# Waiting for every four or five gathers before the next are issued, in a DLRM tower with a compressed interaction network

## The chip, the core and the metric

The kernel runs on one core of a Trainium2 chip. The time is device microseconds from start to end of one execution. The core has a matrix engine (PE, TensorE), a vector engine (DVE, VectorE), an activation engine (ACT, ScalarE), GpSimd (POOL), a queue engine (SP, SyncE) and 16 DMA engines. Each engine runs its own list of instructions, and they meet through semaphores.

## The reference

```python
e = stack([tbl_f[ids[:, f]] for f in range(26)], axis=1)      # (512, 26, 32), tables of 1000 to 125000 rows
x1 = einsum('bik,bjk,hij->bhk', e, e, W1) + b1                # W1 (128, 26, 26)
x2 = einsum('bik,bjk,hij->bhk', x1, e, W2) + b2               # W2 (128, 128, 26)
z = sum(concatenate([x1, x2], axis=1), axis=-1)               # (512, 256)
h = relu(concatenate([z, dense_ctx], axis=1) @ W_top1 + b_top1)   # 272 -> 512
h = relu(h @ W_top2 + b_top2)                                 # 512 -> 256
y = h @ W_top3                                                # (512, 1)
```

Everything is in float32.

## The kernel before

**Batch tiles.** The 512 samples are four tiles of 128. For each tile, GpSimd gathers the 26 embedding rows of its 128 samples: 26 indirect DMAs (L199), each of which brings 128 rows of 128 bytes (one per partition) from one table. The four tiles' buffers `rows[t]` are separate, so no gather waits for a consumer. GpSimd does nothing else after two short instructions (L190, L192): it waits for the indices (`s_idx`) and issues 104 gathers in one go. Each gather adds 16 to `s_got[t][part]`. The fields are in three parts, `PARTS`: 0 to 12, 13 to 22, 23 to 25.

**Setup.** Weights come in over SP's and ACT's queues. Meanwhile and afterwards W1 and W2 are folded into one weight set, independent of the samples. PE walks a list of 37 steps, `SETUP`: 13 steps `fold` (four matmul records each, L219), 5 steps `ctA` and 5 `ctB` (L224, six records each, the last of either two), then transposes `v0` and `v1` (L230, L233). Each step writes one of seven PSUM banks (`RING`), adds 1 to `s_su`, and ACT evicts it (`take`, L345 to L359) and adds 1 to `s_sf`; PE waits for the eviction seven steps back. DVE adds terms of the evicted weights (`add`, L497): first after all 13 folds, then after `ctA`, then after `ctB`.

**A tile.** `half_a(t)` on DVE waits for part 0 (L450), transposes it (L451), copies it (L457), spreads it (L459) and forms products (L608 to L613). `half_b(t)` does so with parts 1 and 2 and makes eight products (L623). PE's `moments(t)` (L252, L253) start with the first of these, in 4 steps that ACT (`evict`, L373 and L381) and DVE (`bands`, L486) evict. Then come `z2_low`, `z2_high`, `z1` (L259 to L272), `layer1(t)` (L283 to L288), and, inside the next tile or at the end, `layer2` (L298) and `layer3` (L305). DVE's order is: setup sums of the folds and of `ctA`, `half_a(0)`, sums of `ctB`, `half_b(0)`, `bands(0)`, and then for each tile `half_a`, `half_b`, `bands`.

Of the kernel before, what the change touches and what calls it, by code (L numbers as in the profile page):

```python
# [71 lines left out]


PARTS = [(0, 13, COL_A), (13, 23, COL_B), (23, 26, COL_B + 10)]

WARM = 24
D_CTX = 16
# [18 lines left out]
def dlrm_tower(nc, io, tables, out):  # L96
    with ExitStack() as ctx:
# [3 lines left out]
        def sem(name):  # L101
            return ctx.enter_context(nc.semaphore(name))
# [40 lines left out]
        s_got = [[sem(f"s_got{t}_{part}") for part in range(3)] for t in range(TILES)]  # L143
# [31 lines left out]
        @block.sync  # L175
        def _(sp):
            sp.dma_start(idx[:, 0, :], io["ids"][:, 0, :]).then_inc(s_idx[0], 16)
            sp.dma_start(w1p[:], io["w1p"]).then_inc(s_w1p, 16)
            sp.dma_start(idx[:, 1:TILES, :], io["ids"][:, 1:TILES, :]).then_inc(s_idx[1], 16)
            sp.dma_start(w2t[:, 0:HALF, :], io["w2t"][:, 0:HALF, :]).then_inc(s_w2, 16)  # L180
            sp.dma_start(wt1[:], io["W_top1"][0:2 * H, :].rearrange("(c p) n -> p c n", p=P)).then_inc(s_wt, 16)
            sp.dma_start(wt1c[:], io["W_top1"][2 * H:2 * H + D_CTX, :]).then_inc(s_wt, 16)
            sp.dma_start(wt2[:], io["W_top2"].rearrange("(c p) n -> p c n", p=P)).then_inc(s_wt, 16)
            sp.wait_ge(s_y, TILES)
            sp.dma_start(out.rearrange("(o b) c -> o (b c)", o=1), y[:]).then_inc(s_out, 16)
            sp.wait_ge(s_out, 16)

        @block.gpsimd
        def _(pool):
            nc.gpsimd.memset(ones[:], 1.0).then_inc(s_ident, 1)  # L190
            pool.wait_ge(s_ident, 1)
            nc.gpsimd.affine_select(out=ident[:], in_=ones[:], compare_op=ALU.is_equal, fill=0.0, base=0,  # L192
                                    pattern=[[-1, P]], channel_multiplier=1).then_inc(s_ident, 1)
            for t in range(TILES):
                if t < 2:
                    pool.wait_ge(s_idx[t], 16)
                for part, (f0, f1, _) in enumerate(PARTS):
                    for f in range(f0, f1):
                        pool.indirect_dma_start(  # L199
                            rows[t][:, f, :], None, tables[f],  # L200
                            bass.IndirectOffsetOnAxis(ap=idx[:, t, f:f + 1], axis=0)).then_inc(s_got[t][part], 16)

        @block.tensor
        def _(pe):
# [212 lines left out]
        def _(dve):  # L417
# [28 lines left out]
            def fields_in(t, part):  # L446

                f0, f1, col = PARTS[part]
                n = f1 - f0
                dve.wait_ge(s_got[t][part], 16 * n)  # L450
                nc.vector.transpose(prod[:, :, col:col + n].rearrange("p g f -> p f g"),  # L451
                                    rows[t][:, f0:f1, :]).then_inc(s_turn[part], 1)
                dve.wait_ge(s_turn[part], t + 1)
                if part == 1:
                    dve.wait_ge(s_pa, t + 1)
                first = f0 % HALF
                nc.vector.tensor_copy(factor[:, :, first:first + n], prod[:, :, col:col + n]).then_inc(s_fac, 1)  # L457
                for r in range(QUADS):
                    nc.vector.tensor_scalar(diag[:, :, f0:f1, r], prod[:, :, col:col + n], quad[:, r:r + 1], None, ALU.mult)  # L459

            def half_a(t):
                if t:
                    dve.wait_ge(s_mom, t * STEPS)
                fields_in(t, 0)
                dve.wait_ge(s_fac, t * len(PARTS) + 1)
                products_a(nc.vector, prod, factor).then_inc(s_pa, 1)

            def half_b(t):
# [4 lines left out]
                dve.wait_ge(s_dup, t + 1)  # L473
                dve.wait_ge(s_fac, (t + 1) * len(PARTS))
                for s in range(PRODS):
# [126 lines left out]
def products_a(eng, prod, factor):  # L602

    def field(f, n=1):
        return prod[:, :, COL_A + f:COL_A + f + n]

    for col, o, d, n in PC + PD:
        eng.tensor_tensor(prod[:, :, col:col + n], factor[:, :, o:o + n], field(o + d, n), ALU.mult)  # L608
    eng.tensor_tensor(prod[:, :, PCD:P11].rearrange("p g (c d) -> p g c d", d=D[1]),
                      with_dims(factor[:, :, C[0]:], (HALF, GROUPS), (1, C[1]), (0, D[1])),  # L610
                      with_dims(field(D[0]), (PCOLS, GROUPS), (0, C[1]), (1, D[1])), ALU.mult)
    for x, col in ((JLOW, P11), (JLOW + 1, P12)):
        ins = eng.tensor_tensor(prod[:, :, col:col + x + 1], factor[:, :, 0:x + 1],  # L613
                                with_dims(field(x), (PCOLS, GROUPS), (0, x + 1)), ALU.mult)
    return ins
# [84 lines left out]
```

## Time and profile before

| | us |
|---|---|
| median of 3 runs | 290.71 (289.09 to 292.08) |
| the profiled execution | 289.82 |
| its span, first to last instruction | 288.1 |
| mean granted clock of TensorE | 0.738 of full speed |

Busy time over the span: PE 161.0 us (56%), DVE 97.5 us (34%), ACT 56.7 us (20%), GpSimd 100.1 us (35%). No engine is busy for much more than half of the span, so the averages do not say what bounds the kernel. The slices of the page and the chain of waits do: the first says when each engine works, the second what released it.

### The profile page before, as it was taken

The numbers are of one execution on the slowest core, as the hardware profiler recorded it, in microseconds if no ns is written. First come the engines' busy times: TensorE is split into PE (matmuls) and PEld (weight loads), VectorE is DVE, ScalarE is ACT, GpSimd is POOL, SyncE is SP. The second block draws the span as 40 slices with busy tenths as digits, with TensorE's granted clock in tenths as the row PEclk, the third lists the DMA queues.
The fourth block names the chain that finished last, engine by engine and source line by source line (L and its number), as shares of the span: only waits on it lengthen the run. The fifth ranks groups of instructions, "written<-read, shape, count | busy, mean of one in ns | idle before, by whom it ended". The sixth has DMA issues, their size and how long they took to land.

```text
span 288.1 us, 3079 instructions
## 1 busy us (share of the span) xinstructions
PE 161.0 (56%) x1193; PEld 146.8 (51%) x1193; DVE 97.5 (34%) x341; ACT 56.7 (20%) x156; POOL 100.1 (35%) x110
## 2 busy tenths in 40 slices
PE   8764221121111111111114449799999999999996
PEld 8753221011010101011014339799999999999995
DVE  2400000000000302100019996499249826973100
ACT  1021000000000000000032423602450245026312
POOL 5777777777777777774000000000000000000000
PEclk9995555555555555555555769979999999999999
DMA  6910110001101101100000000000000000000000
GB/s 228 354 17 12 14 15 14 12 14 14 14 12 14 14 11 15 14 13 9 0 0 0 0 0 3 1 2 0 2 0 2 0 2 1 2 0 2 2 0 0
DMA packets 5217, 5.97 MB, mean 21 GB/s; under 512 B 2226, under 2 KB 4402, under 8 KB 5203
## 3 DMA queue, kind: packets, MB, share of 16 engines
q0 software_dynamic: 3328, 1.71, 4.2%
q1 hardware_dynamic: 1410, 2.52, 2.7%
q10 hardware_dynamic: 464, 1.54, 1.5%
q8 instruction: 9, 0.15, 0.2%
q14 instruction: 6, 0.04, 0.0%
HBM read 5.77 MB, written 0.00 MB: 20 GB/s over the span
## 4 chain that ended last, share of the span: by engine, by line
PE 42%; another core or an unknown queue 35%; DVE 8%; issue 8%; ACT 3%; DMA 3%; SPq 0%
PE bank L252 12%; PE bank L253 6%; PE bank L259 5%; PE bank L263 4%; DVE folded L497 4%; PE bank L219 3%; DMA w2t<-in_w2t_dram 3%; PE bank L266 3%; PE bank L298 3%; PE bank L285 2%; PE bank L283 2%; ACT folded L345 1%; DVE diag L459 1%; PE bank L288 1%
## 5 line engine op out<-in xcount | busy, mean ns | idle before, releaser
L199 POOL DMA_INDIRECT rows<-in_tbl_dram,idx x104 | 99.4, 956 | 32.9 <-issue 31.4
L224 PE MATMUL bank<-w1s,w2t 128*128 128x169 f32 x52 | 21.9, 473 | 100.4 <-issue 97.1
L224 PEld LDWEIGHTS bank<-w1s,w2t 128*128 128x128 f32 x52 | 14.5, 301 | 107.4 <-issue 103.6
L252 PE MATMUL bank<-diag,prod 128*128 128x108 f32 x256 | 49.3, 293 | 1.4 <-DVE prod L623 1.4
L497 DVE TENSOR_TENSOR folded<-folded 128x6 f32<-128x6 f32 (+15 forms) x44 | 5.6, 177 | 108.6 <-issue 99.5
L252 PEld LDWEIGHTS bank<-diag,prod 128*128 128x128 f32 x256 | 38.8, 192 | 1.8 <-ACT v L351 1.8
L253 PE MATMUL bank<-diag,prod 128*77 128x64 f32 x256 | 36.9, 226 | 0.0
L253 PEld LDWEIGHTS bank<-diag,prod 128*77 128x77 f32 x256 | 30.9, 148 | 0.0
L486 DVE COPY t<-bank 13x128 f32<-13x128 f32 (+1 forms) x64 | 16.8, 263 | 31.7 <-PE bank L253 31.0
L345 ACT COPY folded<-bank 128x366 f32<-128x366 f32 x13 | 6.0, 465 | 84.1 <-remote 65.4
L373 ACT COPY t<-bank 55x256 f32<-55x256 f32 (+2 forms) x48 | 14.1, 294 | 28.2 <-PE bank L253 27.9
L497 DVE TENSOR_TENSOR folded<-folded,ct 128x52 f32<-128x52 f32 (+13 forms) x51 | 11.2, 299 | 24.5 <-ACT ct L348 24.5
L459 DVE TENSOR_SCALAR diag<-prod,quad 128x416 f32<-128x416 f32 (+2 forms) x48 | 16.9, 467 | 0.0
L259 PE MATMUL bank<-t,v 128*128 128x128 f32 x104 | 14.3, 301 | 1.8 <-ACT t L381 1.8
L348 ACT COPY ct<-bank 128x507 f32<-128x507 f32 (+1 forms) x10 | 4.7, 548 | 53.2 <-remote 36.1
L381 ACT COPY t<-bank 128x432 f32<-128x432 f32 x32 | 14.8, 514 | 0.0
L259 PEld LDWEIGHTS bank<-t,v 128*128 128x128 f32 x104 | 13.5, 213 | 2.5 <-ACT t L381 2.5
L623 DVE TENSOR_TENSOR prod<-bank,prod 128x364 f32<-128x364 f32 x32 | 14.5, 525 | 0.0
L219 PE MATMUL bank<-w1s,w2t 128*128 128x183 f32 x52 | 10.8, 359 | 6.4 <-issue 4.4
L230 PE MATMUL bank<-ident,folded 128*128 128x128 f32 x26 | 6.0, 422 | 13.1 <-DVE folded L497 13.1
L219 PEld LDWEIGHTS bank<-w1s,w2t 128*128 128x128 f32 x52 | 9.0, 210 | 7.9 <-issue 7.5
L263 PE MATMUL bank<-t,v 128*128 128x128 f32 x104 | 12.6, 278 | 0.0
(55 smaller groups left out, 168.3 us busy)
## 6 DMA issues: line engine op xcount, KB each, us to landing
rows<-in_tbl_dram,idx POOLq DMA_INDIRECT x104
wt<-in_W_top_dram SPq DMA_DIRECT2D x2, 512.0 KB
w2t<-in_w2t_dram ACTq DMA_DIRECT2D x1, 832.0 KB
w2t<-in_w2t_dram SPq DMA_DIRECT2D x1, 832.0 KB
w1t<-in_w1t_dram ACTq DMA_DIRECT2D x1, 640.0 KB
w1p<-in_w1p_dram SPq DMA_DIRECT2D x1, 521.0 KB
idx<-in_ids_dram SPq DMA_DIRECT2D x1, 39.0 KB
dctx<-in_dctx_dram ACTq DMA_DIRECT2D x1, 32.0 KB
```

The lines of the kernel that those rows point to most:

```text
L199: pool.indirect_dma_start(rows[t][:, f, :], None, tables[f], bass.IndirectOffsetOnAxis(ap=idx[:, t, f:f + 1], axis=0)).then_inc(s_got[t][p ...
L219: mm = nc.tensor.matmul(ps[:, i * PAIRS:(i + 1) * PAIRS], w2t[:, x0 + i, :], w1s[:, 0:PAIRS], start=True, stop=True)
L224: mm = nc.tensor.matmul(ps[:, i * CROSS:(i + 1) * CROSS], w2t[:, lo + x0 + i, :], w1s[:, c0:c0 + CROSS], start=True, stop=True)
L252: nc.tensor.matmul(m0[:, a0:a0 + JW * QUADS], prod[:, G, 0:P], mov, start=True, stop=True)
L253: mm = nc.tensor.matmul(m1[0:M1, a1:a1 + J1 * QUADS], prod[:, G, P:P + M1], mov[:, JLOW * QUADS:], start=True, stop=True)
L259: nc.tensor.matmul(Z2[:, 0:P], v0[:, j, :], t0[:, j, :], start=j == 0, stop=False)
L263: nc.tensor.matmul(Z2[:, 0:P], v0[:, j, :], t0[:, j, :], start=False, stop=False)
L381: ins = nc.scalar.copy(t0[:, :, n:n + NBANK].rearrange("p j (g r) -> p j g r", r=QUADS), src)
L459: nc.vector.tensor_scalar(diag[:, :, f0:f1, r], prod[:, :, col:col + n], quad[:, r:r + 1], None, ALU.mult)
L486: ins = nc.vector.tensor_copy(t1[p0:p0 + HALF, GRAM + slot:GRAM + slot + nb, n].rearrange("p j (g r) -> p j g r", r=QUADS), m1[64:64 + HAL ...
L497: ins = nc.vector.tensor_tensor(dest, dest, term[second], ALU.add)
L623: return eng.tensor_tensor(dst, left, right, ALU.mult)
```

## The change

A tuple of field numbers is added, and two waits on GpSimd. Within a tile GpSimd issues the gathers of fields 0 to 4, waits until these have landed, then of 5 to 8, 9 to 12, 13 to 17, 18 to 22 and 23 to 25, with a wait after each group: six groups of 5, 4, 4, 5, 5 and 3 in a tile, 24 in all. The last wait of a tile stands before the first gather of the next. Nothing else differs: gathers, their order, their destinations and semaphores are those of before.

```diff
 PARTS = [(0, 13, COL_A), (13, 23, COL_B), (23, 26, COL_B + 10)]
+
+
+PAUSES = (5, 9, 13, 18, 23, 26)
...
                 for part, (f0, f1, _) in enumerate(PARTS):
                     for f in range(f0, f1):
+                        if f in PAUSES and f > f0:
+                            pool.wait_ge(s_got[t][part], 16 * (f - f0))
                         pool.indirect_dma_start(
                             rows[t][:, f, :], None, tables[f],
                             bass.IndirectOffsetOnAxis(ap=idx[:, t, f:f + 1], axis=0)).then_inc(s_got[t][part], 16)
+                    if f1 in PAUSES:
+                        pool.wait_ge(s_got[t][part], 16 * (f1 - f0))
```

## Rows read from the trace of the kernel before

**Rows 1.** The page's 40 slices of 7.2 us: busy tenths, and the granted clock.
```profile
PE   8764221121111111111114449799999999999996
POOL 5777777777777777774000000000000000000000
PEclk9995555555555555555555769979999999999999
```
**Rows 2.** Chain that ended last, in order of time: start, us, what.
```profile
49.29 10.71 another core or an unknown queue
60.03 0.46 ACT folded L345
...
127.98 0.58 ACT ct L348
...
144.09 0.58 ACT ct L348
```
**Rows 3.** Timeline of ACT: start, us, engine, line, what [idle before <-releaser].
```profile
17.16 0.47 ACT L345 COPY folded<-bank 128x366 f32<-128x366 f32 x1 [0.96 <-PE bank L219]
...
22.12 0.47 ACT L345 COPY folded<-bank 128x366 f32<-128x366 f32 x1 [2.36 <-issue]
...
48.83 0.47 ACT L345 COPY folded<-bank 128x366 f32<-128x366 f32 x1 [10.73 <-remote]
...
149.03 2.93 ACT L348 COPY ct<-bank 128x507 f32<-128x507 f32 x7 [4.35 <-remote]
```
**Rows 4.** Timeline of PE while the gathers run (same columns).
```profile
11.79 6.78 PE L219 MATMUL bank<-w1s,w2t 128*128 128x183 f32 x40 [1.88 <-DMA w2t<-in_w2t_dram]
...
132.17 0.44 PE L224 MATMUL bank<-w1s,w2t 128*128 128x169 f32 x1 [2.35 <-issue]
```
**Rows 5.** Timeline of GpSimd: the 1st, 5th, 7th, 74th and 104th gather.
```profile
2.86 1.14 POOL L199 DMA_INDIRECT rows<-in_tbl_dram,idx  x1 [1.49 <-DMA idx<-in_ids_dram]
...
8.06 0.94 POOL L199 DMA_INDIRECT rows<-in_tbl_dram,idx  x1 [0.30 <-issue]
...
10.56 1.44 POOL L199 DMA_INDIRECT rows<-in_tbl_dram,idx  x1 [0.30 <-issue]
...
94.84 1.24 POOL L199 DMA_INDIRECT rows<-in_tbl_dram,idx  x1 [0.30 <-issue]
...
132.76 0.94 POOL L199 DMA_INDIRECT rows<-in_tbl_dram,idx  x1 [0.30 <-issue]
```
**Rows 6.** Stretches: us, busy (count) of PE, PEld, DVE, ACT, POOL; PEclk, DMA share, GB/s.
```profile
13.00:14.00 1.00, 1.00 (x8) 1.00 (x7) 0.00 (x0) 0.00 (x0) 0.69 (x2) 1.00 1.10 311
...
134.20:134.60 0.40, 0.00 (x0) 0.00 (x0) 0.00 (x0) 0.00 (x0) 0.00 (x0) 0.50 0.21 41
134.60:135.00 0.40, 0.03 (x1) 0.00 (x0) 0.00 (x0) 0.00 (x0) 0.00 (x0) 0.50 0.01 0
```
**Rows 7.** The same view for the slow stretch, the rest of the setup, and tile 1.
```profile
18.00:149.00 131.00, 26.13 (x68) 17.65 (x66) 5.60 (x44) 6.39 (x13) 87.65 (x93) 0.51 0.09 12
149.00:172.80 23.80, 9.40 (x42) 8.42 (x41) 22.77 (x86) 9.60 (x23) 0.00 (x0) 0.60 0.00 0
...
200.30:227.50 27.20, 27.20 (x252) 26.14 (x251) 18.03 (x56) 9.52 (x29) 0.00 (x0) 1.00 0.00 1
```
**Rows 8.** Timeline: last part's transpose and first moments of tile 0, moments of tile 3.
```profile
170.90 0.32 DVE L451 STREAM_TRANSPOSE prod<-rows 128x96 f32<-128x96 f32 x1
...
172.85 0.44 PE L252 MATMUL bank<-diag,prod 128*128 128x108 f32 x2 [1.40 <-DVE prod L623]
...
255.56 0.37 PE L252 MATMUL bank<-diag,prod 128*128 128x108 f32 x2
```
**Rows 9.** Chain in order of time: `z2_low` of tile 0 and of tile 1.
```profile
187.18 4.80 PE bank L259 x26
...
215.34 3.15 PE bank L259 x26
```
**Rows 10.** The page's group of DVE's spreading: count | busy, mean ns | idle before.
```profile
L459 DVE TENSOR_SCALAR diag<-prod,quad 128x416 f32<-128x416 f32 (+2 forms) x48 | 16.9, 467 | 0.0
```

## Prediction

> **What bounds the kernel now.** I read the page's slices first. PE is at one tenth or two from about 25 to 155 us, GpSimd is at seven tenths in just that stretch, and PE is full from 190 us on [rows 1]. So 130 us pass in which no compute engine works, and then the four tiles run one after another, bound by PE: tile 1 takes 27.2 us of which PE is busy 27.2 [rows 7]. In the slow stretch, 18 to 149 us, PE has only 26.1 us of work, at half clock [rows 7].
>
> The chain of waits says what holds that stretch: not the gathers' data (nothing waits for `rows`) but gaps of 10.71, later 15.5 us, between one ACT eviction and the next, put down to no known queue [rows 2]. The timelines give the rule in the gaps. ACT's evictions of fold steps come at 48.83 and 60.03, that is 11.20 us apart [rows 2, 3]. A fold step is four matmul records and four weight loads on PE, and 11.20/8 = 1.40 us. For `ctA` steps it is six and six: evictions at 127.98 and 144.09 [rows 2], 16.1 us, or 11.5 times 1.40. PE itself issues one matmul and one weight load per 2.35 + 0.44 = 2.79 us [rows 4], again 1.40 for each. PE ran its folds early (40 records by 18.6 us, [rows 4]), yet ACT is told of them one by one until 94 us. So what is slow is not the arithmetic but the reporting of finished instructions: each gets through at one per 1.40 us, and PE stops when too many wait.
>
> What is served in those 1.40 us? The gathers are issued every 1.25 us from 2.86 to 132.76 [rows 5]. 104 x 1.40 = 145.6, and 2.86 + 145.6 = 148.5; the stretch ends at 149.03, when ACT does seven evictions in 2.93 us [rows 3]. My reading: each gather leaves 1.40 us of work in something that also carries the engines' finish reports, and takes it at 1.25 us per gather. It falls behind by 0.15 us with each one, 104 x 0.15 = 15.6 us in all, which is the 16.3 us that the slow stretch outlasts the last issue. The start supports this: with few gathers behind it a fold step got through in 0.96 + 0.47 = 1.43 us (the eviction at 17.16 with the idle time before it), at 22.12 in 2.36 + 0.47 = 2.8, at 48.83 in 11.20 [rows 3]. So the price of a report grows with the backlog: 0.18 us at 10 gathers, 0.35 at 16, 1.40 from 37 on at the latest. (A gather is issued every 1.25 us: (132.76 - 8.06)/99 = 1.26 [rows 5].)
>
> **The change, part by part.** It removes nothing and adds 24 waits, 23 of which delay a later gather. Behind each wait on GpSimd are only gathers; who waits for them is DVE's `half_a` and `half_b`.
>
> *The pause itself.* The last gather is issued at 132.76; its transfers run between 134.2 and 134.6 and are over by 135.0 [rows 6], so 2.2 us from issue to landed. From a landed semaphore to the issue it releases: a wait of GpSimd on the indices appears in rows 5; I take 0.25 us, an estimate from the 0.3 us that lie between any two gathers there. Without a pause the next gather comes after 1.25. A pause costs 2.2 + 0.25 - 1.25 = 1.2 us. The gather after the one earlier wait took 1.14, not 0.94 us [rows 5]: 0.2 more, so 1.4 (low end 1.2).
>
> *The first pause* falls into the weight loads: the DMA engines are still full between 13 and 14 us, at 311 GB/s [rows 6]. The fifth gather is issued at 8.06 [rows 5]; it lands between 10.3 (no queueing) and, estimated, 14.5. I take 13.0, so the sixth comes at 13.3 instead of 9.3: 4.0, and 0.2 for the restart, 4.2 (1.2 to 5.6).
>
> *The rest:* 22 x 1.4 = 30.8 us (low 26.4).
>
> *What runs beside the gathers now.* Before, DVE worked 5.6 us in the slow stretch; now the setup's end (22.8 us) and three tiles of 18 us run there too [rows 7]. The 74th gather took 1.24 instead of 0.94 us, the 7th 1.44 [rows 5]; both were issued while DVE summed two SBUF tiles (L497, L444). 0.3 us for a stretch of 2.5 us of sums (the 74th), on the 17 us of sums in the setup, gives 2 us, 3 with a margin. The Trainium skill (SBUF — State Buffer, "Who interferes with whom") says that an instruction with two SBUF inputs contends with GpSimd's reads; the slow gathers agree.
>
> The last gather then lands at 135.0 + 4.2 + 30.8 + 3.0 = 173.0 us. By the same account the backlog no longer grows: a group of five takes 5 x 1.25 + 1.2 = 7.5 us and leaves 5 x 1.40 = 7.0; of four, 6.2 against 5.6; of three, 5.0 against 4.2. The largest backlog is that of five gathers, below the ten that cost 0.18 us a report. This is the gain.
>
> *Can the rest keep up?* Without the reports' delay, work left at 18 us is 26.1 (PE, half clock, so less) + 23.8 for the end of the setup + three tiles of 27.2 to 27.5 [rows 7]: 18 + 26 + 24 + 82 = 150, against tile 3's data at 173. Tile data arrive every 40 us or so (about 49, 90, 132, 173), so each tile after the first waits for its gathers: tile 2 from 132 to about 161. There is 12 us of slack for reports that are still somewhat slow. So the path to the end goes over GpSimd: last landing, then tile 3.
>
> *The tail.* From the transpose of part 2 to the first moments: 172.85 - 170.90 = 1.95 us [rows 8]. From the moments of tile 3, 255.56, to the end of the span, 288.1: 32.5 us. PE has been idle before it, and the clock was at half (1.2 GHz) whenever PE had hardly worked [rows 1]. `z2_low` after an idle PE took 4.80, not 3.15 us [rows 9], 1.65 more; the moments alone would lose as much again. I take 2.5 us (0 to 4).
>
> Sum, against the profiled execution: 173.0 + 1.95 + 32.5 + 2.5 = 210.0 us of span, and 289.82 - 288.1 = 1.7 around it: 211.7. That execution is 0.9 us below the median; I say 212. The low end, with 1.2, 26.4, 0 and 0: 135.0 + 1.2 + 26.4 + 1.95 + 32.5 + 1.7 = 198.8. The high end of this case: 135.0 + 5.6 + 30.8 + 8 + 1.95 + 32.5 + 4 + 1.7 = 219.6.
>
> **Rivals.**
>
> *A. The slowness is tied to a gather being issued, not to a backlog.* Then the reports stay at 1.40 us as long as gathers go on, and the pauses only stretch them: last landing at 173 instead of 135, 38 us later, and all behind it too: 290.7 + 38 = 329 us. It decides if less than one report per 0.2 us or so comes through in the first gathers of a group. For it: 1.40 and 1.25 are close, and the low rate is the same at 48 and at 144 us. Against it: before 18 us twelve gathers had been issued and PE ran 40 records in 6.78 us [rows 4]; and from 133.7 to 144 nothing was issued and it was still slow. This is the case on the other side, slower than before.
>
> *B. The backlog is only partly drained.* The slack is 0.5 us in 7.5. Reports from a PE at full rate (252 matmul records and as many weight loads in 27.2 us, [rows 7]) need room as well. Then tiles 0 to 2 lag, the gathers still end at 173, and one whole tile more is left: 212 + 27 = 239 us; with two, 266. For it: the thin slack. Against it: the seven evictions one on another once the backlog is gone [rows 3], so reports pass in well under 0.1 us when nothing is ahead.
>
> *C. DVE keeps GpSimd from issuing.* In the tiles DVE spreads fields with a tensor_scalar from SBUF to SBUF, 16.9 us in 48 instructions [rows 10], of which three tiles' share, 12.7 us, now lies beside gathers. If each stands still for all of it: 212 + 13 = 225. Against it: 416 elements take about 0.47 us, one element per 1.1 ns, which does not look like a fast mode. The Trainium skill (SBUF — State Buffer, "Who interferes with whom") states that copy and tensor_scalar in two-port modes block GpSimd fully, and says that this starves the descriptors of gathers. No gather of before ran beside one, so the trace does not tell.
>
> *D. The change does nothing:* the report delay comes from elsewhere and its end at 149 is chance. Then GpSimd ends at 173 with tile data in time for tiles 0 and 1 and nearly for the rest: 291, within 1%.
>
> **How the numbers follow.** My forecast 0.62, B 0.15, C 0.07, A 0.13, D 0.03. The likeliest is 212 us. The range must leave out no more than 2 in 10: it takes the forecast from its low end, 199, all of C, and of B the case of one tile with some spread, to 248; A, D and two tiles of B stay outside (about 0.2). Faster by over 1%: 0.62 + 0.15 + 0.07 = 0.84. Within 1% (what a measurement of this kernel can tell from no change): 0.03. Slower: 0.13.
>
> **What the profile would show.** Right: GpSimd's issues in groups, each pause between two starts about 2.45 us; ACT's fold evictions back to back before 35 us, not 11.20 us apart; PE at the moments of tile 0 before 80 us; PE idle between tiles, waiting for products that wait for gathers, and a last gather at about 171; the clock's stretches at half level short. Wrong: by A, evictions still 1.40 us per record after 50 us; by B, PE waiting in small gaps through all the tiles and still at tile 2 when the last gather lands; by C, gathers of well over 1 us beside L459. If the pauses are longer than 2.45 us, 23 of them carry the error straight into the time.

## The result, and the profile after

| | us |
|---|---|
| before, median of 4 runs | 289.9 (288.33 to 292.08) |
| after, median of 4 runs | 219.6 (216.9 to 219.89) |
| ratio after/before | 0.755, 95% interval 0.747 to 0.763 |
| the profiled execution of after, and its span | 219.88, 218.1 |
| mean granted clock | 0.844 |

The gain stands for the chip it was measured on. The kernel before takes 290 us on some chips and 185 us on others, the changed kernel 219 to 220 us on both kinds, so the change makes it 24% faster on the first and 20% slower on the second. I call them chips of the first and of the second kind; whether it is the chip or the hour could not be told apart (in order of time: 290 for the measurement above, 185 to 187 on two further chips, 290 to 291 on three more).

The page of the kernel after, same three lines as in [rows 1], slices of 5.5 us:

```profile
PE   7589939150697499509997970299999105999995
POOL 5535588655755575556656575555675650000000
...
PEclk9969995857579979955999998579999755699999
```

The 130 us in which PE stood at one or two tenths are gone. GpSimd now works at three to eight tenths until 180 us, and PE has a hole ahead of each tile, the last of them at 170 to 182 us.

The timeline of ACT, start, us, what [idle before <-releaser], against [rows 3]:

```profile
14.67 0.46 ACT L352 COPY folded<-bank 128x366 f32<-128x366 f32 x1 [0.76 <-PE bank L226]
15.39 0.47 ACT L352 COPY folded<-bank 128x366 f32<-128x366 f32 x1 [0.26 <-PE bank L226]
...
16.63 0.47 ACT L352 COPY folded<-bank 128x366 f32<-128x366 f32 x1 [0.16 <-issue]
...
21.59 0.47 ACT L352 COPY folded<-bank 128x366 f32<-128x366 f32 x1 [0.16 <-PE bank L226]
```

Fold evictions follow each other at 0.62 us; the last starts at 21.59 instead of 93.63. All of the setup's evictions but the last four are done by 40 us.

The chain that ended last is GpSimd's, start, us, what:

```profile
8.17 5.59 DMA rows<-in_tbl_dram,idx
14.02 0.95 POOL rows L204
...
66.21 2.33 DMA rows<-in_tbl_dram,idx
...
178.05 2.46 DMA rows<-in_tbl_dram,idx
```

Before, no row of the chain in the slow stretch was a gather [rows 2]; now gathers and waits for their landing make 67% of it. The last gather is issued at 178.05 and landed by 180.5.

The timeline where the last part of tile 3 lands:

```profile
180.54 0.34 DVE L458 STREAM_TRANSPOSE prod<-rows 128x96 f32<-128x96 f32 x1 [2.91 <-DMA rows<-in_tbl_dram,idx]
...
182.51 0.73 PE L259 MATMUL bank<-diag,prod 128*128 128x108 f32 x2 [12.75 <-DVE prod L630]
```

From the transpose to the first moments 1.97 us, as in [rows 8] (1.95), and from there to the end 218.1 - 182.5 = 35.6 us. The first moments run at half clock (0.73 us for a pair of records that took 0.37 in [rows 8]), after 12.75 us of idle PE.

### The profile page after: what moved, and what is told of

Read it like the earlier page. It is cut to its first block, busy times and chain, and to the rows that moved or that the text cites. A ratio compares the mean times of both kernels' runs of the same rounds, so it can differ in the third digit from the quotient of the medians.

```text
span 218.1 us, 3081 instructions
## 1 busy us (share of the span) xinstructions
PE 155.6 (71%) x1193; PEld 149.4 (68%) x1193; DVE 97.1 (45%) x341; ACT 56.6 (26%) x156; POOL 110.1 (50%) x110
## 4 chain that ended last, share of the span: by engine, by line
POOL 40%; DMA 28%; PE 15%; issue 15%; DVE 1%; ACT 0%; POOLq 0%
POOL rows L204 40%; DMA rows<-in_tbl_dram,idx 27%; PE bank L259 5%; PE bank L260 2%; PE bank L305 2%; PE bank L266 1%; PE bank L270 1%; PE bank L273 1%; DMA idx<-in_ids_dram 1%; PE bank L312 1%; PE bank L292 0%; PE bank L290 0%; PE bank L295 0%; PE bank L279 0%; DVE diag L466 0%
## 5 line engine op out<-in xcount | busy, mean ns | idle before, releaser
L204 POOL DMA_INDIRECT rows<-in_tbl_dram,idx x104 | 109.4, 1052 | 68.2 <-DMA rows<-in_tbl_dram,idx 42.2
L259 PE MATMUL bank<-diag,prod 128*128 128x108 f32 x256 | 59.2, 332 | 40.4 <-DVE prod L630 39.2
L259 PEld LDWEIGHTS bank<-diag,prod 128*128 128x128 f32 x256 | 46.2, 226 | 41.5 <-issue 40.1
L260 PE MATMUL bank<-diag,prod 128*77 128x64 f32 x256 | 41.1, 247 | 0.0
L260 PEld LDWEIGHTS bank<-diag,prod 128*77 128x77 f32 x256 | 36.3, 171 | 0.0
L458 DVE STREAM_TRANSPOSE prod<-rows 128x416 f32<-128x416 f32 (+2 forms) x12 | 7.8, 653 | 43.4 <-DMA rows<-in_tbl_dram,idx 43.4
L466 DVE TENSOR_SCALAR diag<-prod,quad 128x416 f32<-128x416 f32 (+2 forms) x48 | 17.1, 487 | 0.0
L266 PEld LDWEIGHTS bank<-t,v 128*128 128x128 f32 x104 | 13.4, 212 | 5.0 <-ACT t L388 4.8
L237 PEld LDWEIGHTS bank<-ident,folded 128*128 128x128 f32 x26 | 5.3, 227 | 11.0 <-issue 11.0
L270 PEld LDWEIGHTS bank<-t,v 128*128 128x128 f32 x104 | 11.9, 192 | 0.7 <-issue 0.7
L226 PEld LDWEIGHTS bank<-w1s,w2t 128*128 128x128 f32 x52 | 9.4, 217 | 3.5 <-issue 3.5
L504 DVE TENSOR_TENSOR folded<-folded,ct 128x52 f32<-128x52 f32 (+13 forms) x51 | 11.2, 296 | 0.5 <-ACT ct L355 0.4
L504 DVE TENSOR_TENSOR folded<-folded 128x6 f32<-128x6 f32 (+15 forms) x44 | 4.3, 173 | 10.9 <-ACT folded L352 10.8
```

The lines of the kernel that those rows point to most:

```text
L204: pool.indirect_dma_start(rows[t][:, f, :], None, tables[f], bass.IndirectOffsetOnAxis(ap=idx[:, t, f:f + 1], axis=0)).then_inc(s_got[t][p ...
L226: mm = nc.tensor.matmul(ps[:, i * PAIRS:(i + 1) * PAIRS], w2t[:, x0 + i, :], w1s[:, 0:PAIRS], start=True, stop=True)
L259: nc.tensor.matmul(m0[:, a0:a0 + JW * QUADS], prod[:, G, 0:P], mov, start=True, stop=True)
L260: mm = nc.tensor.matmul(m1[0:M1, a1:a1 + J1 * QUADS], prod[:, G, P:P + M1], mov[:, JLOW * QUADS:], start=True, stop=True)
L266: nc.tensor.matmul(Z2[:, 0:P], v0[:, j, :], t0[:, j, :], start=j == 0, stop=False)
L270: nc.tensor.matmul(Z2[:, 0:P], v0[:, j, :], t0[:, j, :], start=False, stop=False)
```

## The experiments

**The two kernels once more, on another chip.** Both unchanged.

> The kernel before, unchanged, to have its trace beside the changed kernel's on one chip. In the last runs it took 186.7 us on another chip than the 290 us of its first measurement. Backlog theory: what a gather leaves to be served takes more than the 1.25 us issue spacing in one condition of the machine (1.40) and less in the other. If the chip of this run is as the first, 290 us and evictions 11.2 us apart; if as the second, 187 us, evictions under 1 us apart until 25 us, and never a slow stretch: nothing in between, unless the service time lies within a few hundredths of 1.25.

Measured: 184.7 us (183.64 to 185.77, 2 runs; with the others of that chip 184.94, 182.07 to 186.94, 7 runs). The page of this run of the kernel before, and its timeline of ACT:

```profile
PE   6949994910699959999999953999999389999994
...
POOL 4777778878777777777777777777777300000000
```
```profile
14.92 0.46 ACT L345 COPY folded<-bank 128x366 f32<-128x366 f32 x1 [0.76 <-PE bank L219]
16.14 0.46 ACT L345 COPY folded<-bank 128x366 f32<-128x366 f32 x1 [0.76 <-PE bank L219]
16.84 0.46 ACT L345 COPY folded<-bank 128x366 f32<-128x366 f32 x1 [0.24 <-PE bank L219]
```

The same program, gathers issued every 1.25 us in the median just as in [rows 5] (1.34 in the mean, against 1.26 there, since DVE now works beside them), and no slow stretch. The two chips part at 16 us: here evictions go from 1.22 to 0.70 and 0.62 us apart, there from 1.43 to 2.8 and on to 11.2. The last gather is issued at 141.37 and the span ends 40.5 us later.

> The changed kernel, unchanged. Backlog theory: its time does not depend on the condition, since its mean spacing is above 1.40 us: 217 to 220 us on any chip. So it is faster where the kernel before takes 290 and slower by 17% (219/187) where that takes 187. Rival (the chips differ in all they do): it is faster here in proportion, about 141 us.

Measured: 219.53 us (218.97 to 220.79, 4 runs), ratio to before on this chip 1.204 (1.191 to 1.218). Last issue at 177.21, end 40.0 us later. I had expected a ratio of 219/187 = 1.17. So the time of the changed kernel is that of its gathers, on either chip; what changes is what it is compared with.

**Spacing without a wait.** A scratch tile is cleared ahead of each gather, with 320 or 96 columns; there is no wait for a landing.

```diff
                     for f in range(f0, f1):
+                        if gaps:
+                            pool.wait_ge(s_gap, gaps)
+                        nc.gpsimd.memset(pad[:], 0.0).then_inc(s_gap, 1)
+                        gaps += 1
                         pool.indirect_dma_start(
```

On the second kind of chip:

> The kernel before, no waits for landings; ahead of each gather GpSimd clears a scratch tile of 320 columns, which should space the gathers by more than 1.40 us (I estimate 1.6 to 1.7, from the 0.20 us that its memset of 128 columns took). Backlog theory: a spacing above 1.40 us is all that is needed, so ACT's fold evictions come back to back before 35 us, and the end is the last landing plus 37 us: with a spacing s, 3 + 104 s + 2.2 + 37, so 209 us at 1.6 and 219 at 1.7. Rival (GpSimd must stand and wait until nothing is in flight, or the delay hangs on a gather being issued at all): evictions 11 us apart as before, and a time over 300 us.

> As e1, but the scratch tile has 96 columns. e1's gathers came every 1.50 us with 320 columns (memset of 0.25 us or so hidden in part), last landing near 168. With 96 I expect 1.33 to 1.45 us. If the chip serves a gather in 1.40 us and the spacing is 1.42 or more: about 195 us. If the spacing is below 1.40: reports slow towards the end, 200 to 290. On a chip without a slow stretch: 3 + 104 x 1.35 + 2.2 + 37 + 2 = 185 to 196 us, no faster than the kernel before.

Measured: 207.5 us (1 run, before 186.66) and 193.24 us (190.8 to 194.0, 4 runs, before 184.94), gathers every 1.50 and 1.31 us (medians, here and below, unless a mean is named). No slow stretch in either, but there was none to remove: on such a chip each makes the kernel slower by what it delays the last gather. The ends are 39.1 and 40.2 us after the last issue (166.66, 150.67).

On the first kind:

> e1's kernel once more: gathers every 1.50 us, no wait for a landing. Where the kernel before takes 290: backlog theory says that 1.50 is above 1.40, so there is no slow stretch at all (evictions 0.62 to 1.2 us apart) and 207 us, as on the other chip, where 1.31 us gave 266.5; the rival (a full stop is needed, spacing only helps in part) says over 230. Where the kernel before takes 185: 207 us under both, and nothing is told apart.

> e7's kernel once more, on whatever chip this is. Where the kernel before takes 185: again 191 to 194 us, last issue plus 40 us, since its gathers come every 1.31 us and, with those that DVE delays, 1.43 in the mean. Where the kernel before takes 290: spacing of 1.43 in the mean is just above 1.40, of 1.31 below; backlog theory gives 193 to 230 us, the rival (only a full stop helps) 290 or more.

Measured: 209.2 us (208.08 to 210.32, 2 runs; before 290.72), ratio 0.721 (0.707 to 0.735), with 1.50 us; 266.52 us (266.43 to 266.61, 2 runs; before 290.13), ratio 0.919 (0.913 to 0.925), with 1.31 us. ACT with 1.50 us, and then with 1.31:

```profile
16.42 0.46 ACT L352 COPY folded<-bank 128x366 f32<-128x366 f32 x1 [0.16 <-PE bank L226]
17.04 0.47 ACT L352 COPY folded<-bank 128x366 f32<-128x366 f32 x1 [0.16 <-issue]
...
66.68 0.90 ACT L380 COPY t<-bank 55x256 f32<-55x256 f32 x3 [4.26 <-remote]
```
```profile
30.22 0.47 ACT L352 COPY folded<-bank 128x366 f32<-128x366 f32 x1 [4.47 <-remote]
35.88 0.46 ACT L352 COPY folded<-bank 128x366 f32<-128x366 f32 x1 [5.19 <-remote]
42.91 0.47 ACT L352 COPY folded<-bank 128x366 f32<-128x366 f32 x1 [6.57 <-remote]
52.04 0.46 ACT L352 COPY folded<-bank 128x366 f32<-128x366 f32 x1 [8.66 <-remote]
61.87 0.47 ACT L352 COPY folded<-bank 128x366 f32<-128x366 f32 x1 [9.37 <-remote]
```

These two runs tell the theories apart. With 1.50 us one to two gathers are always in flight and GpSimd never waits for a landing, yet the setup is fast and the kernel ends 39.8 us after its last issue (168.77), as with the 24 full stops. Reports are not all on time even so: in tiles 0 to 2 most evictions of the moments come 5 to 6 us apart (the row at 66.68 is one; `remote` there means that the profile names no instruction that released it), where the same kernel has 3.1 on the second kind. It costs next to nothing, because each tile waits for its gathers anyway. With 1.31 the slow stretch is there and comes later: 5.7, 7.0, 9.1, 9.8 us between evictions where the kernel before had 7.7 and then 11.2 from 37.63 us on. A slower growth of the backlog (0.09 instead of 0.15 us a gather) does just that. But 266.5 us lies between what I had written down for the two sides, 193 to 230 and 290 or more. I had taken the mean spacing, which DVE's delays raise to 1.43 us on both kinds, as the one to hold against 1.40; a mean above 1.40 did not save this kernel. GpSimd's own reports can be late too: five of its memsets here waited 0.8 to 1.5 us for the one before.

**A spacing next to the threshold.** The same edit with 232 columns, on the first kind.

> Gathers spaced by a scratch tile of 232 columns: 1.31 us at 96 and 1.50 at 320 give 1.42 here. Where the kernel before takes 290: just above 1.40, so if the threshold lies there, no slow stretch, last issue at about 3 + 103 x 1.42 + 10 for the gathers that DVE delays = 159, plus 40 and 1.7: 201 us, the fastest of all on such a chip. If the threshold is nearer 1.5, a growing gap between evictions and 220 to 265 us. Where the kernel before takes 185: 201 us.

Measured: 228.46 us (226.72 to 231.46, 4 runs; before 290.76), ratio 0.784 (0.779 to 0.789), spacing 1.42 us. The profiled execution took 231.46 us. The evictions in its timeline:

```profile
33.08 0.30 ACT L355 COPY ct<-bank 128x169 f32<-128x169 f32 x1 [0.17 <-remote]
36.69 0.58 ACT L355 COPY ct<-bank 128x507 f32<-128x507 f32 x1 [3.30 <-remote]
...
90.01 0.91 ACT L380 COPY t<-bank 55x256 f32<-55x256 f32 x3 [9.81 <-remote]
```

The folds are fast up to 22 us, then gaps of 3 us come, and in the tiles gaps of up to 13.3. So 1.42 is not above the threshold for a core whose engines work at full rate: my 201 us was wrong by 27. The last issue is at 161.10, near the 159 expected, but the end is 68.6 us later, not 40. That is what rival B of the prediction describes: gathers leave 1.40 us each, and the reports of PE at full rate need room besides. The reading is argued from the numbers; what a report needs was not measured. For this kernel the spacing from which the end is that of the gathers lies between 1.42 and 1.50 us, or, with the gathers that DVE delays, between 1.53 and 1.61 us in the mean.

**Fewer pauses.** The changed kernel with groups of 13, two pauses in a tile.

```diff
-PAUSES = (5, 9, 13, 18, 23, 26)
+PAUSES = (13, 26)
```

> The changed kernel with pauses only after fields 12 and 25: groups of 13. Mean spacing (13 x 1.25 + 1.36)/13 = 1.355 us, below 1.40. Backlog theory: it falls behind by 0.6 us in each group and 1.8 within one, to about 5 us at the end, so reports get slow from some 50 us on (0.3 to 1 us each); the end lies between the changed kernel and the one before, about 250 us (230 to 280). Rival (a pause clears whatever it is, however few there are): the reports stay fast, the last gather lands 17 pauses of 1.36 us earlier than at 180.4, at 157, and the time is 157 + 37 + 2 = 196 us.

> e2's kernel once more: two pauses in a tile, 1.355 us in the mean while nothing else delays gathers, 1.25 within a group. Where the kernel before takes 290: below 1.40, so the backlog grows by 0.15 us in each gather and is cut by 1.36 us in each pause, some 0.6 us more per group: reports slow from about 40 us on, less than at 1.31 us (266.5): 215 to 260 us. Rival (a stop to an empty queue resets it): 195 us as on the other chip. Where the kernel before takes 185: 195 us.

Measured: 194.98 us on the second kind (1 run, before 186.66), 268.9 us on the first (265.31 to 272.49, 2 runs, before 290.72; the profile is of the 265.31). My range there ended at 260, and the mean spacing was 1.41 us, not 1.355. ACT on the first kind, around the second pause (from 36.19 to 38.86 us):

```profile
31.62 0.46 ACT L352 COPY folded<-bank 128x366 f32<-128x366 f32 x1 [1.68 <-PE bank L231]
34.44 0.47 ACT L352 COPY folded<-bank 128x366 f32<-128x366 f32 x1 [2.35 <-remote]
42.20 0.58 ACT L355 COPY ct<-bank 128x507 f32<-128x507 f32 x1 [7.30 <-remote]
53.48 0.58 ACT L355 COPY ct<-bank 128x507 f32<-128x507 f32 x1 [10.70 <-issue]
```

GpSimd stands until nothing is in flight, and the reports are still slower after it than before it. The landings themselves are on time: all seven pauses take 2.56 to 2.67 us from one start to the next, 2.56 to 2.65 where nothing else delays them on the second kind. A full stop does not reset what is behind; its length counts, and some 1.36 us in 13 gathers are too few. The rival (195 us) is out, on the kind of chip where it matters.

**One tile's gathers.** The kernel before with 26 gathers only, on the second kind; all tiles compute on tile 0's rows.

```diff
-            for t in range(TILES):
+            for t in range(1):
                 if t < 2:
...
-                dve.wait_ge(s_got[t][part], 16 * n)
+                dve.wait_ge(s_got[0][part], 16 * n)
                 nc.vector.transpose(prod[:, :, col:col + n].rearrange("p g f -> p f g"),
-                                    rows[t][:, f0:f1, :]).then_inc(s_turn[part], 1)
+                                    rows[0][:, f0:f1, :]).then_inc(s_turn[part], 1)
```

> The kernel before with only tile 0's 26 gathers; all four tiles compute on tile 0's rows (so 78 gathers are left out and three tiles' results are not theirs). Backlog theory: 26 x 1.40 us of work from 2.9 us on, so the slow reports end by about 39 us, wherever the setup is then; then the rest at full speed: tile 0 from about 60, 60 + 27.5 + 27.2 + 27.3 + 33.3 = 175 us of span, 177. Rival (the setup itself is slow, gathers or not): ACT evictions 11 us apart after 40 us and the time near 290.

Measured: 168.11 us (1 run, before 186.66). Not a test of the backlog, since there was none on that chip. It shows what the engines take when no tile waits for its rows, moments of tile 0 from 49.78 us on. On the second kind of chip the kernel before is thus bound by its gathers already, by 186.66 - 168.11 = 18.6 us, and every delay of GpSimd goes into the time.

**Other traffic beside the gathers.** The kernel before, and SP loads 110 times 128 rows of 128 bytes into scratch, on the first kind.

```diff
+            sp.wait_ge(s_wt, 48)
+            for k in range(110):
+                b = k % 2
+                if k >= 2:
+                    sp.wait_ge(s_junk[b], 16 * (k // 2))
+                sp.dma_start(junk[b][:], io["W_top1"][0:128, 0:32]).then_inc(s_junk[b], 16)
```

> The kernel before, and beside its gathers SP loads 110 times 128 rows of 128 bytes into a scratch tile that nobody reads, two in flight (a load about every 1.1 us, until some 130 us). Backlog theory: what serves the gathers and the engines' reports also carries other transfers' packets; 128 more per 1.1 us on top of a gather's 32 per 1.25 us push it over, and a slow stretch of gaps appears on a chip that has none (evictions well over 1 us apart after 20 us, over 230 us in all); where the kernel before is at 290 it gets slower still. Rival (the slow stretch belongs to the chip, or to GpSimd's own queue, and other traffic has no part in it): the time stays within 3% of the kernel before on the same chip.

Measured: 289.06 us (1 run), before 290.13. Its page's DMA line, and ACT:

```profile
DMA packets 21058, 7.78 MB, mean 27 GB/s; under 512 B 18066, under 2 KB 20242, under 8 KB 21043
```
```profile
51.19 0.46 ACT L355 COPY folded<-bank 128x366 f32<-128x366 f32 x1 [10.73 <-remote]
62.39 0.47 ACT L355 COPY folded<-bank 128x366 f32<-128x366 f32 x1 [10.74 <-remote]
...
149.33 3.21 ACT L358 COPY ct<-bank 128x507 f32<-128x507 f32 x7 [7.21 <-remote]
```

Four times the packets (the loads ran until 155 us), and still 11.20 us between evictions and an end of the stretch at 149.33 instead of 149.03. This part of my theory fell: what serves the gathers' 1.40 us does not carry these loads' packets, or does so at no price that shows.

**Half the bytes.** The kernel before with rows of 64 bytes, on the first kind.

```diff
+            for t in range(TILES):
+                link(nc.vector.memset(rows[t][:, :, EMB // 2:EMB], 0.0))
...
-                            rows[t][:, f, :], None, tables[f],
+                            rows[t][:, f, 0:EMB // 2], None,
+                            tables[f].rearrange("v (a b) -> (v a) b", a=2),
```

> The kernel before, each gather bringing rows of 64 bytes instead of 128 (the tables are seen as twice as many half rows; the other half of each buffer is filled with zeros by DVE, so other numbers are summed). As many rows and packets, half the bytes. Where the kernel before takes 290: if the 1.40 us are paid by the row or by the gather, evictions stay 11.2 us apart and the time at 290; if by the byte, there is no slow stretch and 185 us. Where the kernel before takes 185: 185 us, and nothing is told of the 1.40 us.

Measured: 285.0 us (1 run, before 290.76). An earlier form (e4), which left the other half of each buffer unwritten, gave no time.

```profile
55.40 0.46 ACT L346 COPY folded<-bank 128x366 f32<-128x366 f32 x1 [10.73 <-issue]
66.60 0.46 ACT L346 COPY folded<-bank 128x366 f32<-128x366 f32 x1 [10.74 <-issue]
```

11.20 us again: the 1.40 us are paid by the gather or by its 128 rows, not by the byte. The 5.8 us that it is faster are not a faster report: seven folds instead of five were evicted by 22.2 us, before the gaps grew, so tile 0's moments start at 166.70 instead of 172.85.

## Why the prediction was right, point by point

**The slow stretch and its cause.** Forecast: finish reports get through at one per 1.40 us because gathers are issued faster than something serves them, and a mean spacing above 1.40 ends it. The first half is borne out on the first kind of chip; that the spacing sets the lateness is shown by changing it in two ways:

| kernel, first kind | spacing, median | mean | us | end after last issue |
|---|---|---|---|---|
| before | 1.25 | 1.26 | 290 | 155.3 |
| two pauses in a tile | 1.25 | 1.41 | 268.9 | 115.3 |
| memset of 96 columns | 1.31 | 1.43 | 266.5 | 114.0 |
| memset of 232 columns | 1.42 | 1.53 | 228.5 | 68.6 |
| memset of 320 columns | 1.50 | 1.61 | 209.2 | 39.8 |
| six pauses in a tile (the change) | 1.25 | 1.70 | 219.6 | 40.0 |

Spacings and ends are those of the profiled executions. Ordered by the mean spacing, pauses and memsets make one row down to the 40 us of a kernel without lateness: it does not matter how the room is made. The backlog account also dates the end of the lateness. If each gather takes 1.40 us, from its start or from the end of the one before, whichever is later, the backlog is gone at 154.4 us with 96 columns and at 150.8 with two pauses, 3.6 and 2.5 us after the last issue instead of 15.7; the last of ACT's late evictions come at 154.28 and 151.05. With 232 columns the same sum never shows a backlog of gathers, and reports are late all the same: there it is too simple.

The second half was wrong: means of 1.41, 1.43 and 1.53 us are above 1.40 and still slow, since the prediction's sum gave the reports no room of their own. The changed kernel was far enough above, 1.70, and even in it two of the moments' evictions in tile 0 come 5.4 and 4.8 us after the one before instead of 3.1 to 3.4. The forecast's own times make a mean of (173.0 - 2.2 - 2.9)/103 = 1.63 us, close to where the series turns. That this margin is enough, no step of it had worked out; to that extent it was luck.

What serves the gathers is not shown; plain loads of SP and the bytes of a gather are excluded. Open as well is why some chips have it and others not, and, the rival that no run tested, whether it belongs to the kernel or to its recording: every time here is of an execution whose span and clock were recorded.

**Rival A** (tied to the issue of a gather, 329 us) is out: 104 gathers are issued in all of these kernels.

**The last landing.** Forecast 173.0, measured 180.5. Term by term: the first pause cost 4.6 us (forecast 4.2); the 22 others 30.6, or 1.39 each (30.8, 1.4). The sizes are right, but not the parts: gathers after a wait took 0.94 to 0.97 us (but one beside DVE's sums), not the 1.14 of the first in [rows 5], and landing and restart took the rest (66.21 to the next start at 68.80 is 2.59 us, forecast 2.45). The landing of the last took 2.46 instead of 2.2.

**The term that was mis-sized is what DVE does to GpSimd:** forecast 3 us, measured 10.0, and with it nearly all of the 7.5 us by which the last landing was late. It is the difference of GpSimd's busy time in gathers (109.4 against 99.4). The timeline beside the slow ones, GpSimd and DVE:

```profile
27.63 3.16 POOL L204 DMA_INDIRECT rows<-in_tbl_dram,idx  x1 [2.25 <-DMA rows<-in_tbl_dram,idx]
...
118.04 2.02 POOL L204 DMA_INDIRECT rows<-in_tbl_dram,idx  x1 [0.30 <-issue]
```
```profile
27.00 5.43 DVE L504 TENSOR_TENSOR folded<-folded,ct 128x65 f32<-128x65 f32 x26 [0.40 <-ACT ct L355]
...
118.08 1.85 DVE L466 TENSOR_SCALAR diag<-prod,quad 128x416 f32<-128x416 f32 x4
```

I had scaled by sums of tiny tiles, 0.3 us in 2.5. The larger sums of two SBUF tiles, which ran after the last gather in the kernel before, more than triple one gather. Over the 0.945 us of an undisturbed gather, about 7 us arise up to 51 us, and 3.9 in the tiles, beside the spreading (L466); in the kernel before it was 1.1 in all. That is rival C in small: not the 12.7 us for which it would have stood still, but 0.4 to 1.1 us for each group of four. The Trainium skill (SBUF — State Buffer, "Who interferes with whom") has copy and tensor_scalar in two-port modes block GpSimd, and sums of two SBUF inputs contend with its reads. For the sums the trace agrees (3.16 us against 0.94). Beside the spreading it shows a delay, but of at most 1.1 us in the 1.85 that four instructions take, and in which mode L466 runs no run here shows. On the second kind of chip the kernel before pays DVE's delays as well (GpSimd busy 108.5 us in gathers).

**The tail.** Forecast 1.95 + 32.5 + 2.5 = 37.0, measured 37.6: from tile 3's first moments to the end it took 35.6 instead of 32.5 us, 3.1 more, within the 0 to 4 that I had kept open for the clock after an idle PE.

**Rival B** (tiles lag by one, 239 us) did not come for 24 pauses: PE waited for products, not for reports, ahead of each tile. In part it was there: late reports inside tiles 0 and 1 cost 2.3 and 1.6 us more than on the second kind (first to last eviction of the moments, 11.8 and 10.8 against 9.5 and 9.2), which the wait for the next gathers hid. At a spacing of 1.42 us it came in full: tile 1, begun at 106.9, still runs at 163 us, when the last gather has landed, and two more tiles follow (moments at 169.9 and 197.2). With the seven evictions one on another I had shown that reports are cheap one by one, but not that their sum finds room; the pauses' mean spacing of 1.70 us leaves it.

**What no step of the prediction had** is that 290 us was one of two levels of the kernel before. Nothing in one trace shows it. The last issue plus 40 us (39.1 to 40.5 us in seven profiles of both kinds that have no slow stretch or next to none) gives the span of each of them. For the kernel before, 132.76 would make it 173 against its 288.1, but with the reports on time DVE delays its gathers: on the second kind the last issue is at 141.37 and the span 181.9. So about 106 us was the whole of what could be won, and the change wins 70.

**A version for both kinds** was not found. On the first, spacing at 1.50 us without waits beats both kernels (209.2 against 290.7 and 219.6). On the second the kernel before stays the fastest (184.9 against 193.2, 195.0, 207.5 and 219.5).

## What to carry to other kernels

If all engines crawl at one common step per instruction while GpSimd gathers, compare that step with the gathers' spacing: the cure is the spacing, not the wait, and it has to leave room for the reports too: here a mean of 1.61 us was enough for a step of 1.40 and cost least, a mean of 1.53 was not. Measure such a change on several chips before keeping it, since here the same edit gave 0.755 and 1.204. When work moves beside gathers, price GpSimd's delay by the largest SBUF operations that will run there, not by the small ones that already do.

## What the runs showed of the hardware

- The same program took 290 us on four occasions and 185 to 187 us on two, and in the profiles of both levels gathers are issued every 1.25 us in the median. What differs at first is the finish reports of the engines: 1.40 us for each of PE's instructions against too little to see.
- On the first kind of chip the reports of PE, DVE and (in one run) GpSimd are late, while the landings of gathers are not: with two pauses in a tile the wait for them stayed at 2.56 to 2.67 us from start to start, with ACT's evictions over 10 us apart.
- A gather of 128 rows costs GpSimd 0.94 us, up to 3.2 beside sums of two SBUF tiles on DVE, and 1.4 to 2.0 beside a group of four spreads.
